# Another order for ScalarE and POOL in a convolution with divisive normalisation

## The reference

```python
pooled = x.mean(axis=(2, 3))
t = relu(gamma * (pooled @ w1.T - running_mean) * rsqrt(running_var + 1e-5) + beta)
wt = (t @ w2.T + b2).reshape(b * 96, 1, 3, 3) * MASK     # only 4 of 9 taps: row above, and left
out = conv(x, wt, padding 1, one group per image and channel) + bias
# second layer
denom_sq = einsum('nchw,ic->nihw', out * out, gamma_eff) + beta_eff
result = out * rsqrt(denom_sq)
```

## Time and profile before

| | us |
|---|---|
| median of 3 runs (213.76 to 215.5) | 213.86 |
| the profiled execution's own time | 215.21 |
| its span, first to last instruction | 213.3 |
| VectorE busy | 187.5 |
| TensorE busy | 174.7 |
| ScalarE busy | 161.9 |
| POOL busy | 149.3 |

### The profile page before, as it was taken

How to read it: one execution, slowest core, us unless ns; L and a number is a source line. 1 busy time by engine, 2 the same in 40 slices (tenths; PEclk the granted TensorE clock), 3 DMA queues, 4 the chain that set the end, 5 groups by cost and what they waited for, 6 DMA issues and landing times.

```text
span 213.3 us, 2851 instructions
## 1 busy us (share of the span) xinstructions
PE 174.7 (82%) x986; PEld 65.4 (31%) x986; DVE 187.5 (88%) x183; ACT 161.9 (76%) x176; POOL 149.3 (70%) x79
## 2 busy tenths in 40 slices
PE   0018794789899999897999998989999989859981
PEld 0015541233253323232533232325432323112220
DVE  3798699997999899999998999999989999999173
ACT  2335492948986999999869999998695858692692
POOL 2000033358897899999998999999988798892800
PEclk9999999969999999999999999999999999995998
DMA  6999939816989899979999999846374647377387
GB/s 200 419 412 405 413 128 337 267 25 182 338 298 332 294 343 377 387 267 333 327 312 366 325 367 404 281 160 210 134 224 174 217 149 244 131 246 246 108 289 221
DMA packets 16580, 58.09 MB, mean 272 GB/s; under 512 B 2387, under 2 KB 2390, under 8 KB 16566
## 3 DMA queue, kind: packets, MB, share of 16 engines
q1 hardware_dynamic: 14256, 51.72, 65.6%
q10 hardware_dynamic: 2310, 6.19, 11.1%
HBM read 26.45 MB, written 25.17 MB: 242 GB/s over the span
## 4 chain that ended last, share of the span: by engine, by line
ACT 22%; DVE 22%; PE 18%; POOL 17%; issue 9%; DMA 7%; ACTq 3%; SPq 1%; DVEq 0%; POOLq 0%
DVE psum L592 10%; POOL work L643 10%; PE psum L542 8%; POOL work L637 7%; ACT work L455 7%; DVE y L592 5%; ACT work L428 5%; ACT psum L420 4%; DMA ximg<-in_x 4%; ACT pool_out L369 4%; PE psum L471 3%; ACTq L437 3%; DMA par_s<-in_par 2%; PE psum L526 2%; PE psum L553 2%
## 5 line engine op out<-in xcount | busy, mean ns | idle before, releaser
L643 POOL TENSOR_TENSOR work<-y,work 128x1024 f32<-128x1024 f32 x44 | 103.9, 2376 | 12.4 <-ACT work L455 12.4
L592 DVE SCALAR_TENSOR_TENSOR psum<-ximg,taps,psum 128x1024 f32<-128x1024 f32 x81 | 104.3, 1288 | 7.2 <-ACT psum L420 4.2
L542 PE MATMUL psum<-work,gam_e 96*32 96x512 f32 x540 | 86.5, 621 | 11.6 <-ACT work L455 6.8
L543 PE MATMUL psum<-sqd,gam_e 96*32 96x512 f32 x180 | 86.2, 622 | 0.0
L637 POOL TENSOR_TENSOR work<-y 128x1024 f32<-128x1024 f32 x24 | 45.4, 1892 | 40.0 <-DVE y L592 40.0
L592 DVE SCALAR_TENSOR_TENSOR y<-ximg,taps,psum 128x1024 f32<-128x1024 f32 x47 | 60.2, 1281 | 1.7
L526 PE MATMUL psum<-ximg,diag 128*128 128x512 f32 x120 | 58.0, 606 | 0.0
L455 ACT ACTIVATE work<-psum,beta_e 128x1024 f32<-128x1024 f32 x45 | 49.5, 1099 | 9.5 <-PE psum L543 9.5
L369 ACT ACTIVATE pool_out<-ximg 128x1935 bf16<-128x1935 f32 (+2 forms) x22 | 40.9, 1858 | 9.1 <-DMA ximg<-in_x 8.3
L542 PEld LDWEIGHTS psum<-work,gam_e 96*32 96x32 f32 x540 | 22.5, 113 | 70.9 <-issue 66.8
L420 ACT ACTIVATE psum<-ximg,par_s,taps 128x1024 f32<-128x1024 f32 x32 | 38.4, 1199 | 0.5
(11 more groups left out here) (61 smaller groups left out, 51.6 us busy)
## 6 DMA issues: line engine op xcount, KB each, us to landing
out_y<-work SPq DMA_DIRECT2D x45, 512.0 KB, 3.5
ximg<-in_x SPq DMA_DIRECT2D x36, 516.0 KB, 6.5
ximg<-in_x SPq DMA_DIRECT2D x12, 580.5 KB, 8.0
sqd<-work ACTq DMA_DIRECT2D x45, 128.0 KB, 3.6
out_y<-work SPq DMA_DIRECT2D x2, 384.0 KB, 3.3
out_y<-work SPq DMA_DIRECT2D x4, 192.0 KB, 2.6
par_s<-in_par ACTq DMA_DIRECT2D x1, 281.0 KB, 5.2
sqd<-y SPq DMA_DIRECT2D x2, 128.0 KB, 3.0
```

Of the source, the lines that this page charges most:

```text
L542: nc.tensor.matmul(den(n)[own, j:j + BANK], gam_e[:, own], held(n)[0:C, j:j + BANK], start=True, stop=True)
L543: ins = nc.tensor.matmul(den(n)[C:P, j:j + BANK], gam_e[:, s * CD:(s + 1) * CD], sqd[:, t % 2, j:j + BANK], start=True, stop=True)
L592: return nc.vector.scalar_tensor_tensor(out=in_rows(dst), in0=tap_in(n, tap), scalar=tap_w(b, s, tap), in1=in_rows(src), op0=ALU.mult, op1 ...
L643: nc.gpsimd.tensor_tensor(held(n), result(n), held(n), ALU.mult).then_inc(scaled, 1)
```

## The change

It writes ScalarE's loop and POOL's loop in another order. On ScalarE the base of slot 1 of unit t moves from the end of iteration t-1 into iteration t, behind the square and the two moves of the unit before; the two pools of a unit no longer stand together; move(t,0) stands ahead of the second pool and of square(t,1). On POOL the two squares of a unit move behind the scales of slots 1 and 2 of unit t-2. TensorE's loop starts its round at another point, and the tap sums stand between the two halves of slot 2's base. The burst of six matmuls and the wait for a root ahead of the last full denominators are removed. The two last squares of the fourth quarter are made on VectorE, with a semaphore of their own.

```diff
         def square_last(act, k):
             n, lo, hi = LAST_PARTS[k]
-            if n == FOURTH:
-                act.wait_ge(fourth_moved[0], 16 * SLOTS)
-                if lo > 0:
-                    act.wait_ge(fourth_moved[1], 16)
-            else:
-                act.wait_ge(convolved, n + 2 if lo > 0 else n + 1)
+            act.wait_ge(convolved, n + 2 if lo > 0 else n + 1)
...
-        def base_on_pe(pe, n):
+        def base_on_pe(pe, n, halves):
...
-            for j in range(N // BANK):
+            for j in halves:
...
-            ins.then_inc(based_pe, 1)
+            if j == N // BANK - 1:
+                ins.then_inc(based_pe, 1)
...
         def denominators_last(pe, k):
-            pe.wait_ge(squared, squares(LAST - 1) + k + 1)
+            if n == FOURTH:
+                pe.wait_ge(squared_fourth, 2 if lo > 0 else 1)
+            else:
+                pe.wait_ge(squared, squares(LAST - 1) + k + 1)
...
+        def square_fourth(dve, k):
+            n, lo, hi = LAST_PARTS[k]
+            dve.wait_ge(fourth_moved[0], 16 * SLOTS)
+            if lo > 0:
+                dve.wait_ge(fourth_moved[1], 16)
+            wait_stored(dve, n)
+            nc.vector.tensor_tensor(held(n)[0:C, lo:hi], fourth[:, lo:hi], fourth[:, lo:hi], ALU.mult).then_inc(squared_fourth, 1)
...
             read_other_taps(act)
-            base_on_act(act, 1)
             diagonals(act, 0)
             for t in range(UNITS_ALL - 1):
                 b, u = divmod(t, UNITS)
                 chain = u == TAPS_UNIT and b < B - 1
+                rsqrt(act, at(t - 2, 1))
+                square(act, at(t - 1, 2))
+                move_d(act, at(t - 1, 1))
                 move_d(act, at(t - 1, 2))
+                base_on_act(act, at(t, 1))
                 rsqrt(act, at(t - 2, 2))
-                pool_next(act, t, 1)
                 if chain:
                     hidden(act, b + 1, t)
-                square(act, at(t, 1))
-                pool_next(act, t, 0)
-                if chain:
                     read_taps(act, b + 1, t)
                     diagonals(act, b + 1)
                 base_on_act(act, at(t + 1, 0))
+                pool_next(act, t, 1)
                 rsqrt(act, at(t - 1, 0))
                 move_d(act, at(t, 0))
-                square(act, at(t, 2))
-                rsqrt(act, at(t - 1, 1))
-                move_d(act, at(t, 1))
-                if t == UNITS_ALL - 2:
-                    move_d(act, LAST - 1)
-                base_on_act(act, at(t + 1, 1))
-            rsqrt(act, LAST - SLOTS - 1)
+                pool_next(act, t, 0)
+                square(act, at(t, 1))
+            rsqrt(act, LAST - 5)
+            square(act, LAST - 1)
+            move_d(act, LAST - 2)
+            move_d(act, LAST - 1)
+            base_on_act(act, LAST + 1)
+            rsqrt(act, LAST - 4)
             base_on_act(act, LAST + 2)
             square_last(act, 0)
             rsqrt(act, LAST - 3)
+            square_last(act, 1)
             rsqrt(act, LAST - 2)
-            square_last(act, 1)
             rsqrt(act, LAST - 1)
-            rsqrt_last(act, 0)
             square_last(act, 2)
             square_last(act, 3)
-            rsqrt_last(act, 1)
-            rsqrt_last(act, 2)
-            square_last(act, 4)
-            square_last(act, 5)
-            for k in range(3, len(LAST_PARTS)):
+            for k in range(len(LAST_PARTS)):
                 rsqrt_last(act, k)
...
-                for s in range(SLOTS):
-                    denominators(pe, at(t - 2, s))
+                denominators(pe, at(t - 2, 2))
                 if chain:
                     hidden_sums(pe, b + 1, t)
...
-                base_on_pe(pe, at(t, 2))
+                base_on_pe(pe, at(t, 2), (0,))
                 if chain:
                     tap_sums(pe, b + 1, t)
+                base_on_pe(pe, at(t, 2), (1,))
+                if chain:
                     pe.wait_ge(taps_ready, b + 2)
-            pe.wait_ge(normed, LAST - SLOTS)
-            keep_awake(SLOTS)
-            for n in range(LAST - SLOTS, LAST):
-                denominators(pe, n)
+                denominators(pe, at(t - 1, 0))
+                denominators(pe, at(t - 1, 1))
+            denominators(pe, LAST - 1)
...
-            for k in range(len(LAST_PARTS)):
+            scale_last(dve, 0)
+            square_fourth(dve, 4)
+            square_fourth(dve, 5)
+            for k in range(1, len(LAST_PARTS)):
                 scale_last(dve, k)
...
-            for t in range(-1, UNITS_ALL):
-                square_on_pool(pool, at(t + 1, 0))
-                scale(pool, at(t - 1, 1))
-                square_on_pool(pool, at(t + 1, 1))
-                scale(pool, at(t - 1, 2))
-                scale(pool, at(t, 0))
+            for t in range(UNITS_ALL):
+                scale(pool, at(t - 2, 1))
+                scale(pool, at(t - 2, 2))
+                square_on_pool(pool, at(t, 0))
+                square_on_pool(pool, at(t, 1))
+                scale(pool, at(t - 1, 0))
+            scale(pool, LAST - 2)
```

More of the change, by code:

```diff
@@ L163, in conv_gdn @@
         squared_pool = sem("squared_pool")
+        squared_fourth = sem("squared_fourth")
         d_moved = [sem(f"d_moved{i}") for i in range(2)]
@@ L440, in square_last @@
             n, lo, hi = LAST_PARTS[k]
-            if n == FOURTH:
-                act.wait_ge(fourth_moved[0], 16 * SLOTS)
-                if lo > 0:
-                    act.wait_ge(fourth_moved[1], 16)
-            else:
-                act.wait_ge(convolved, n + 2 if lo > 0 else n + 1)
+            act.wait_ge(convolved, n + 2 if lo > 0 else n + 1)
             wait_stored(act, n)
-            nc.scalar.activation(held(n)[0:C, lo:hi], last_result(n)[:, lo:hi], ACT.Square).then_inc(squared, 1)
+            nc.scalar.activation(held(n)[0:C, lo:hi], result(n)[0:C, lo:hi], ACT.Square).then_inc(squared, 1)
         def rsqrt(act, n):
```

## The result

The changed kernel takes 232.14 us (median of four runs, 228.69 to 235.58) against 213.81; the ratio is 1.083, with an interval of 1.065 to 1.101. It is slower, as forecast, by 18.3 us where 10.5 were forecast. The ratio is taken over the fast executions of both kernels alone, so it is not quite the quotient of the two medians. The profiled execution, whose span follows, took 228.69 us in all; it is the quickest of the four.

What follows compares the result with a forecast made beforehand. It took VectorE's 10.21 us a unit as the floor, with ScalarE as full in pooled units. Start +1.5, 13 units +11.1 and end -2.1 gave +10.5, a median of 224.4 us, range 215 to 236.

Steps and rivals of the forecast that it cites:

- The two places: The order changes on ScalarE, (A), and on POOL, (B), where the prediction put the real change.
- (A): ScalarE: move(t-1,2) waits for the square just ahead, then base(t,1) follows; 1.64 us instead of 0.95, 0.69 more a unit.
- (B): POOL's square(t,0) behind two scales delays move(t,0), the pool and the next base on ScalarE; 11.55 us a pooled unit.
- x: The start of ScalarE's base(t,1), from which the prediction counts times within a unit.
- The start: Pools, square and moves now stand ahead of base(2,1), so its convolution starts at 52.55 instead of 51.04: +1.5 us.
- The end: From unit 15 on, fourth quarter's squares on VectorE and no burst: a gain of 2.1 us taken.
- the upper bound: The end at full clock throughout: squares to 14.8, last product at x + 18.9, a gain of 3.1 us.
- Landings: Arrival of move(t-1,2) before TensorE's denominators: hidden under (B) up to 4.5 us, costed at nothing; longest up to 2 us.
- the 13 units: Slot 1 convolutions from block (2,1) to (15,1) on VectorE: 149.7 us forecast against 138.6, +11.1.
- a rival with 0.8 to 1.5 us a unit: TensorE's clock falls in most units; eleven by 1.2 give 13 us, about 237; chance 0.15.
- a sign of being wrong: Profile sign listed under wrong: TensorE's clock below 1.00 in the middle of the run, pointing to the clock rival.

Runs made afterwards that it cites:

- without landings: Kernels issuing moves from an unchanging tile, TensorE not waiting: changed kernel 231.8 us, only (A) left 216.7, only (B) left 217.9, neither 210.7, kernel before 210.6.
- the late move: Changed kernel with base(t,1) ahead of move(t-1,2) on ScalarE: 239.53 us, ratio 1.126.
- both edits: Changed kernel with POOL's square(t,0) back ahead of the scales of unit t-2, and base(t,1) ahead of move(t-1,2) on ScalarE: 227.48 us.
- the run that was to take the clock out: Changed kernel with six idle matmuls ahead of slot 0's denominators in every unit: 240.71 us, ratio 1.138.

## Why the prediction was right, point by point

**The two places: right, to 0.1 or 0.2 us a unit.** (A) was worked out as 1.64 us from square to base; the trace has 98.53 - 96.89 = 1.64. That an issue holds what is behind it, taken from one row at the start, held in 15 turns. (B) was to end the wait of the pool at x + 7.1; in the unit shown base(t,1) is at 86.88 and the pool at 94.08, 7.2. Units 4 and 5 were to take 11.55 and took 11.63 and 11.65; unit 6 11.77 and 11.85; units 12 to 14 10.7 and 10.8; unit 3 12.0 and 12.2. Taking the places away one at a time without landings gave the order of 10.2, 10.6, 11.0, 11.6 that the working asks for.

**The start: nearly.** +1.5 was forecast; from the first convolution to that of (2,1) the trace has 27.0 us against 25.8, +1.2. From root(0,1) to base(2,1) it has 47.70 to 50.34, 2.64 us where 2.65 was worked out. But the root was taken at 48.65, as before, and came 0.95 earlier: the kernel before had its clock at half there, from 45 to 48. So the agreement of the total is in part luck, and without landings both orders need the same time for this stretch, 24.6 and 24.5 us.

**The end: right in kind, low in size.** From base(15,1) to VectorE's last product, as in the earlier trace rows:

```profile
203.90 1.21 ACT L421 ACTIVATE psum<-ximg,par_s,taps 128x1024 f32<-128x1024 f32 x1 [0.59 <-ACT work L429]
...
217.92 1.29 DVE L636 TENSOR_TENSOR work<-sqd 96x512 f32<-96x512 f32 x2
...
221.47 1.28 DVE L628 TENSOR_TENSOR work<-sqd,work 96x512 f32<-96x512 f32 x2
```

221.47 + 1.28 - 203.90 = 18.9 against 22.0, a gain of 3.1, the upper bound, not the 2.1 that I took. It came although TensorE's clock was at half from 207 to 210: the upper bound was worked out for full clock, and half clock was to cost a part of it. VectorE ended the fourth quarter's squares at x + 15.3, near the 14.8 of the upper bound, and the products follow them. So here the transfers of the fourth quarter more than the clock seem to set the end; no run takes the clock out.

**Landings: right in most units, for a reason that doesn't travel.** They were costed at nothing up to a flight of 4.5 us, since (B) covers them. In units 4 to 6 and 8 to 14 that held: the distances are the same without landings. In unit 2 it didn't: a flight of 5.2 us kept TensorE waiting for 2.8 us, until 55.03, with half clock behind it. The unit lost 0.9 us by it, within the 2 that the prediction gave to a late landing. In all TensorE waited 12.6 us in 7 places. That (B) covers them is true of this kernel alone: with (A) gone and (B) left in place they cost 22 us, with (B) gone 8 and with both gone 17. In the changed kernel no last move took more than 4.9 us from unit 3 on; with the late move and with both edits five took 6.3 to 6.9.

**The clock: the term that was mis-sized.** I gave it no place in the sum of the 13 units, and a rival with 0.8 to 1.5 us a unit and a chance of 0.15. It fell three times in the 13 units: in unit 2, in unit 7, and between 10 and 11 with no cost to be seen. The prediction had named a clock below 1.00 in the middle of the run as a sign of being wrong, and this sign is there. Unit 7, in two stretches of TensorE's timeline, to be read with the earlier trace rows:

```profile
112.00:114.00 2.00, 0.76 (x7) 1.00 0.97 291
114.30:117.60 3.30, 3.30 (x9) 0.52 0.94 329
```

TensorE had been idle for 1.9 us waiting for the hidden values, and then built the second half of slot 2's base at half clock, 3.3 us instead of 1.9. That unit took 13.8 us where unit 3, the same work, took 12.2; unit 2 took 12.7 where 11.8 was told. Against the 12.0 and 11.8 of the forecast these two make 2.8 us of the 3.9 by which the 13 units exceed its 149.7; 0.1 to 0.2 in most of the others makes the rest. In unit 2 the late landing has a share in it. The span came to 226.6, the forecast was 223.8. The median lies higher since most executions lose more: the spans of six executions of the changed kernel are 226.6, 228.9, 229.9, 230.2, 231.6 and 233.4 at a granted clock of 0.956, 0.952, 0.953, 0.945, 0.946 and 0.938. On the whole the lower the clock, the longer the span. That is a correlation; which stretches fell in the slower ones no profile here shows, and the run that was to take the clock out failed to. Of the 7.7 us between 224.4 and 232.1 this is the likely cause and not a shown one. So the forecast has the mechanism of the units and their size, 149.7 against 153.6 us. That the median stays inside its range with 7.7 us more is not the sum's merit but the width's.

The Trainium skill, page "TensorE: Matmul & The Clock Gate", part "HAM oscillation — how this bites in real kernels", describes a loop that waits for a transfer in each turn and starts every turn at half clock. The traces bear that out in part. In the changed kernel idle stretches of 2.5 us (99.8 to 102.3) and 2.4 us (137.6 to 140.0) left the clock at full. In the run with both edits the denominators behind an idle stretch of 3.0 us started at half clock, at 127, and those behind the 3.3 us shown above fell to it within a microsecond. Idle time and half clock together cost these two units 5.2 and 4.3 us, where I had written 1.2 for a turn.

## What to carry to other kernels

Before moving a DMA issue in an engine's hand-written list, ask what its semaphore wait stops behind it: an issue right behind the instruction that makes its data costs the wait and the issue, 0.6 us a turn here, and one that waits for another engine ties that engine's order into the loop. Once several engines stand near the floor, undoing one of two faults can make things worse (239.5 us against 232.1 here); a kernel without the transfer's wait tells lists and flights apart, if the distances of single units are compared and not the totals alone. And a filler for TensorE is only free where the work behind it isn't already late.

## What the runs showed of the hardware that I had not expected

- A late landing with the fall of the clock behind it cost a unit 4 to 5 us: in the run with both edits two units of 10.2 became 15.4 and 14.6. The denominators, the root and the next base stand in one row there, and VectorE's start came 4.3 us late.
- A DMA issue on ScalarE's queue holds the engine for its 0.51 us wherever nothing is running ahead of it: issued at 93.46, with the pool behind it at 94.08, it was paid for, and issued at 95.31, beside the pool of 94.08, it was not. A wait on the engine's own last result costs 0.03 us.
- The flight of 128 KB from ScalarE's queue varies from 2.2 to 7.5 us within one execution, with medians of 2.8 to 3.7 in these runs, and having the loads follow the move did not shorten the longest.
